# Local attention in a two-layer perceiver kernel: the shares of two of five sampling points move from VectorE to GpSimd

## The reference, cut to what matters

```python
loc_x = jnp.mod(ref + off + loc, sign_lens[:, None, None, None])
xg = loc_x / (key_len - 1) * 2.0 - 1.0
ix = ((xg + 1.0) * key_len - 1.0) / 2.0
x0 = jnp.floor(ix); dx = ix - x0
sk = 0.5 * (w0 * _gather_pad0(Kh, i0) + w1 * _gather_pad0(Kh, i1))   # w0 = 1 - dx, w1 = dx
sv = 0.5 * (w0 * _gather_pad0(Vh, i0) + w1 * _gather_pad0(Vh, i1))
scores = jnp.einsum('bhqd,bhqkd->bhqk', Qh / math.sqrt(HD), sk)
attn = jax.nn.softmax(scores, axis=-1)
```

## Time and profile before

| | us |
|---|---|
| median of three timed runs | 2892.89 (2889.31 to 2894.97) |
| profiled execution | 2884.54 |
| its span | 2882.6 |
| what lies around the span | 1.9 |
| VectorE busy, whole span | 1579.4 |
| GpSimd busy, whole span | 1008.7 |
| local attention, its loop over batches | from about 46 to 255 |

### The profile page before, as it was taken

How to read it: one execution, slowest core, us unless ns; L and a number is a source line. 1 busy time by engine, 2 the same in 40 slices (tenths; PEclk the granted TensorE clock), 3 DMA queues, 4 the chain that set the end, 5 groups by cost and what they waited for, 6 DMA issues and landing times. The chain is left out here.

```text
span 2882.6 us, 40247 instructions
## 1 busy us (share of the span) xinstructions
PE 2620.4 (91%) x15816; PEld 2126.3 (74%) x15816; DVE 1579.4 (55%) x2702; ACT 1056.8 (37%) x2114; POOL 1008.7 (35%) x486
## 2 busy tenths in 40 slices
PE   3887789997999999999999999999999868599898
PEld 2554478886888888888888888888888623377777
DVE  4895455443544544544444444444444469766775
ACT  2562223223443444443434434434344344222221
POOL 3561245444524313413432242143120037443342
PEclk7998789998999999999999999999999978799999
DMA  4000011112102111111111121121010000010110
GB/s 93 16 12 1 22 44 56 56 65 73 47 23 81 28 37 56 39 37 45 39 48 45 28 76 29 37 61 39 32 28 1 11 1 0 22 61 27 44 44 15
DMA packets 51501, 109.64 MB, mean 38 GB/s; under 512 B 21376, under 2 KB 26880, under 8 KB 46992
## 3 DMA queue, kind: packets, MB, share of 16 engines
q1 hardware_dynamic: 51344, 107.45, 12.3%
HBM read 106.05 MB, written 1.38 MB: 37 GB/s over the span
## 5 line engine op out<-in xcount | busy, mean ns | idle before, releaser
L1947 PE MATMUL img_ps<-cn,pt_hi 127*128 127x512 f32 x1536 | 552.0, 400 | 8.1 <-POOL cn L1666 8.0
L1948 PE MATMUL img_ps<-cn,pt_lo 127*128 127x256 f32 x1536 | 430.3, 280 | 0.0
L1664 POOL TENSOR_SCALAR ct<-staged 128x762 fp32r<-128x762 f32 x64 | 136.5, 2132 | 756.8 <-DMA staged<-in_ctx_t 526.7
L1947 PEld LDWEIGHTS img_ps<-cn,pt_hi 127*128 127x128 f32 x1536 | 290.0, 189 | 68.0 <-POOL cn L1666 8.2
L2073 DVE TENSOR_TENSOR pt_lo<-t_ps,pt_hi 127x512 fp32r<-127x512 f32 x384 | 241.4, 683 | 137.9 <-ACT pt_hi L2067 137.9
L1924 PE MATMUL s_ps<-ct,a_hi 128*128 128x508 f32 x768 | 312.2, 406 | 0.0
L1926 PE MATMUL s_ps<-ct,a_lo 128*128 128x508 f32 x768 | 301.4, 392 | 0.0
L1925 PE MATMUL s_ps<-ct,a_hi 128*128 128x508 f32 x768 | 301.3, 392 | 0.0
L1948 PEld LDWEIGHTS img_ps<-cn,pt_lo 127*128 127x128 f32 x1536 | 289.8, 189 | 0.0
L2130 ACT ACTIVATE prob<-s_ps,bias 128x1524 f32<-128x1524 f32 x128 | 196.6, 1536 | 142.4 <-DVE bias L2186 142.4
L1547 ACT ACTIVATE gate_e<-g_ps_e 128x512 f32<-128x512 f32 x136 | 81.4, 598 | 429.1 <-PE u_ps_e L1464 429.1
(11 more groups left out here) (327 smaller groups left out, 5784.9 us busy)
## 6 DMA issues: line engine op xcount, KB each, us to landing
staged<-in_ctx_n SPq DMA_DIRECT2D x64, 384.0 KB, 3.2
staged<-in_ctx_t SPq DMA_DIRECT2D x64, 381.0 KB, 3.2
up_raw_w<-in_up SPq DMA_DIRECT2D x17, 1024.0 KB, 4.8
down_raw_w<-in_down SPq DMA_DIRECT2D x17, 512.0 KB, 3.5
w_shared<-in_wq SPq DMA_DIRECT2D x7, 1024.0 KB, 6.2
w_shared<-in_wo SPq DMA_DIRECT2D x7, 1024.0 KB, 4.8
win<-in_ctx_near SPq DMA_DIRECT2D x16, 128.0 KB, 2.1
wv<-in_wv SPq DMA_DIRECT2D x1, 2048.0 KB, 8.7
```

What stands on the lines that cost most here:

```text
L1664: nc.gpsimd.tensor_scalar(hi, piece, 1.0, None, ALU.mult).then_inc(first.hi_done, 1)
L1947: nc.tensor.matmul(img_ps[:], pt_hi[0:IBLK, j, :], rows[0:IBLK, :, j, :], start=j == 0, stop=False)
L1948: last = nc.tensor.matmul(img_ps[:, D:2 * D], pt_lo[0:IBLK, j, :], rows[0:IBLK, 0, j, :], start=False, stop=j == IB - 1)
```

## The change

On GpSimd, the share of the last two points is formed by a new function `share_out`, behind `prepare(b + 1)` in the written order of batch b: it waits for `attn` of batch b (the sixth step of the semaphore `soft`) and for the sums of the same part of the batch before, and then issues the one multiply. VectorE issues the same function for the first three points alone. `share_done` becomes a list of two semaphores, one for each part. `attn` is no longer in the PSUM tile `marks` but in an SBUF array of its own, `attn0`; before VectorE writes it, it waits for GpSimd's share of the batch before. Two semaphores that counted single steps of VectorE, `spread_zeroed` and `half_kept`, become one, `kept_step`. What is computed is the same.

```diff
--- before.py
+++ after.py
@@ -400,7 +400,7 @@
     tent = [sb(f"tent{s}", [P, NK, TILES0, QW]) for s in range(2)]
     hit, share = sb("hit", [P, NK, TILES0, QW]), sb("share", [P, NK, TILES0, QW])
     spread = sb("spread0", [P, TILES0 * (WN + QT)])
-    score, shifted = sb("score", [P, PK]), sb("shifted", [P, PK])
+    score, shifted, attn = sb("score", [P, PK]), sb("shifted", [P, PK]), sb("attn0", [P, PK])
     turned = sb("turned0", [P, H0, S])
     total = sb("total0", [P, TILES0])
     inv = sb("inv0", [P, TILES0])
@@ -410,15 +410,16 @@
     w_ps = [ps(f"w0_ps{g}", [P, 4, P]) for g in range(2)]
     o_ps = ps("o_ps", [P, C, P])
     marks = ps("marks", [P, 512])
-    top, attn, weight = marks[:, 0:TILES0], marks[:, PK:2 * PK], marks[:, 2 * PK:3 * PK]
+    top, weight = marks[:, 0:TILES0], marks[:, 2 * PK:3 * PK]
     win_in = [sem(f"win_in{s}") for s in range(2)]
     kv_done, kt_kept, v_kept, q_masked = sem("kv_done"), sem("kt_kept"), sem("v_kept"), sem("q_masked")
     scored, dist_done, tent_step = sem("scored"), sem("dist_done"), sem("tent_step")
-    hit_done, soft, spread_zeroed = sem("hit_done"), sem("soft_step"), sem("spread_zeroed")
+    hit_done, soft = sem("hit_done"), sem("soft_step")
     exp_done = sem("exp_done")
-    share_done, summed, spread_done = sem("share_done"), sem("summed0"), sem("spread_done")
+    share_done = [sem(f"share_done{h}") for h in range(2)]
+    summed, spread_done = sem("summed0"), sem("spread_done")
     turned_done, turned_kept = sem("turned_done"), sem("turned_kept")
-    out_done, half_kept, out_kept = sem("out_done"), sem("half_kept"), sem("out_kept")
+    out_done, kept_step, out_kept = sem("out_done"), sem("kept_step"), sem("out_kept")
     SOFT = 6
     HALVES = NB // 2
 
@@ -426,6 +427,15 @@
 
     def part(buffer, h):
         return buffer[:, POINTS[h]].rearrange("p n i m -> p (n i m)")
+
+    def tiled(ap):
+        return ap.rearrange("p (a n) -> p a n", n=NK)
+
+    def share_out(eng, s, h):
+        points = POINTS[h].stop - POINTS[h].start
+        eng.tensor_tensor(share[:, POINTS[h]], tent[s][:, POINTS[h]],
+                          tiled(attn[:]).rearrange("p i n -> p n i")[:, POINTS[h]].unsqueeze(3)
+                          .broadcast_to([P, points, TILES0, QW]), ALU.mult).then_inc(share_done[h], 1)
 
     block = ctx.enter_context(nc.Block())
 
@@ -473,7 +483,7 @@
         def sums(b):
             pe.wait_ge(spread_done, b)
             for h in range(2):
-                pe.wait_ge(share_done, b * 2 + (h + 1))
+                pe.wait_ge(share_done[h], b + 1)
                 for n in range(NK)[POINTS[h]]:
                     last = nc.tensor.matmul(sum_ps[:].rearrange("p i m -> p (i m)"), k.ident,
                                             share[:, n].rearrange("p i m -> p (i m)"), start=n == 0, stop=n == NK - 1)
@@ -531,7 +541,7 @@
             pool.wait_ge(k.pos_in[0 if old is None else 1], H0 * 16)
             for h in range(2):
                 if old is not None:
-                    pool.wait_ge(share_done, old * 2 + (h - 1))
+                    pool.wait_ge(share_done[h], old)
                 points = POINTS[h].stop - POINTS[h].start
                 nc.gpsimd.tensor_tensor(
                     tent[s][:, POINTS[h]], small(k, "iota").rearrange("p (i m) -> p i m", m=QW)
@@ -546,6 +556,10 @@
                 b = i * 2 + s
                 if not (last and s == 1):
                     prepare(b + 1, 1 - s, None if first and s == 0 else b)
+                pool.wait_ge(soft, b * SOFT + 6)
+                if b > 0:
+                    pool.wait_ge(summed, b * 2)
+                share_out(nc.gpsimd, s, 1)
 
         pairs_of_batches(pool, body)
 
@@ -580,7 +594,7 @@
         for h in range(2):
             distances(0, 0, h)
             tents(0, 0, h)
-        act.wait_ge(spread_zeroed, 1)
+        act.wait_ge(kept_step, 1)
 
         def body(i, first, last):
             for s in range(2):
@@ -616,8 +630,8 @@
             if not isinstance(b, int) or b > 0:
                 dve.wait_ge(out_kept, b + 0)
             mask = small(k, "mask2")
-            nc.vector.tensor_scalar(kept[:], o_ps[:, :, 0:S], mask[:, 0:1], None, ALU.mult).then_inc(half_kept, 1)
-            dve.wait_ge(half_kept, b + 1)
+            nc.vector.tensor_scalar(kept[:], o_ps[:, :, 0:S], mask[:, 0:1], None, ALU.mult).then_inc(kept_step, 1)
+            dve.wait_ge(kept_step, b + 2)
             nc.vector.scalar_tensor_tensor(out=k.ctx_t[:, :, bass.ds(b * S, S)], in0=o_ps[:, :, S:2 * S],
                                            scalar=mask[:, 1:2], in1=kept[:], op0=ALU.mult,
                                            op1=ALU.add).then_inc(out_kept, 1)
@@ -630,9 +644,6 @@
 
         def by_tile(ap):
             return ap.unsqueeze(2).broadcast_to([P, TILES0, NK])
-
-        def tiled(ap):
-            return ap.rearrange("p (a n) -> p a n", n=NK)
 
         def body(i, first, last):
             for s in range(2):
@@ -661,21 +672,18 @@
                 dve.wait_ge(soft, at + 4)
                 nc.vector.reciprocal(inv[:], total[:]).then_inc(soft, 1)
                 dve.wait_ge(soft, at + 5)
-
-                nc.vector.scalar_tensor_tensor(out=tiled(attn), in0=tiled(weight), scalar=0.5, in1=by_tile(inv[:]),
+                if old:
+                    dve.wait_ge(share_done[1], b)
+                nc.vector.scalar_tensor_tensor(out=tiled(attn[:]), in0=tiled(weight), scalar=0.5, in1=by_tile(inv[:]),
                                                op0=ALU.mult, op1=ALU.mult).then_inc(soft, 1)
                 dve.wait_ge(soft, at + 6)
-                for h in range(2):
-                    if old:
-                        dve.wait_ge(summed, b * 2 + (h - 1))
-                    points = POINTS[h].stop - POINTS[h].start
-                    nc.vector.tensor_tensor(share[:, POINTS[h]], tent[s][:, POINTS[h]],
-                                            tiled(attn).rearrange("p i n -> p n i")[:, POINTS[h]].unsqueeze(3)
-                                            .broadcast_to([P, points, TILES0, QW]), ALU.mult).then_inc(share_done, 1)
+                if old:
+                    dve.wait_ge(summed, b * 2 - 1)
+                share_out(nc.vector, s, 0)
                 if old:
                     keep_outputs(b - 1)
 
-        nc.vector.memset(spread[:], 0.0).then_inc(spread_zeroed, 1)
+        nc.vector.memset(spread[:], 0.0).then_inc(kept_step, 1)
         pairs_of_batches(dve, body)
         keep_outputs(NB - 1)
```

## The result

The changed kernel takes 2910.89 us (median of 4 executions, 2907.52 to 2914.25) where the kernel before took 2891.24 us (median of 4 as well): a ratio of 1.0066, 95% interval 1.0048 to 1.0085, or 19.65 us more. The forecast was 2913 us, 20 us more. The profiled execution of the changed kernel took 2913.36 us, its span 2911.5.

The account below looks back on a forecast made before the run. Three tied paths at 10.9 us a batch were taken to bound the local attention; a new 12.65 us loop through GpSimd costs 19.0 us over 12 batches, plus 1 us for the clock: 2913 us, range 2899 to 2926.

Parts of the forecast that it names:

- The tie: Local attention, kernel before: VectorE, TensorE and ScalarE paths tie at 10.90 us a batch; removing 1.21 us from VectorE gains nothing.
- The queue: GpSimd's written order: masks and tents stand behind its wait and share, closing a new loop of 12.65 us a batch.
- (3): Part on GpSimd's queue place: loop of Exp, attn, GpSimd's share, masks, tent, Abs, spread, Relu, next Exp.
- The turns: Shares reading two SBUF operands exclude each other; VectorE goes first, 1.75 us, GpSimd's ends 1.80 to 1.94 us behind.
- Twelve steps: Local attention: 12 of 13 batch steps lengthen from 11.07 to 12.65 us, 19.0 us in all; the last stays.
- The clock: TensorE idles longer in each batch, so its clock may drop: 1 us added to the forecast.
- The rest of the kernel: Everything behind the local attention stage starts later and is otherwise the same.
- The signs: Expected in the trace: 12.6 us period, GpSimd's share 3.4 to 3.7 us, Exp wait grown 1.7 us, `hit` waiting.
- Side by side: Rival: both shares run without turns, loop 11.12 us a batch, 2894 us, no change that can be told; chance 0.12.
- GpSimd first: Rival: GpSimd's share runs before VectorE's, 11.94 us a batch, 2904 us; chance 0.08.
- A low clock: Rival: TensorE's clock falls and stays low, 15.7 us in half of the batches, 2931 us; chance 0.05.
- VectorE the only bound: Rival: VectorE alone bounds the stage, so the change saves 16 us, 2877 us; chance 0.03.

Follow-up runs that it names:

- edit B: Kernel before, with VectorE's share of the last two points formed for only 1 of 64 keys, nothing added elsewhere: 2888.54 us, ratio 0.9987.
- experiment 1: Changed kernel, with VectorE writing attn a second time into PSUM and its three-point share reading that copy: 2889.57 us, ratio 0.9997.
- experiment 3: Changed kernel, with a PSUM copy of attn for VectorE and the query masks made ahead of GpSimd's wait: 2888.43 us, ratio 0.9992.

## Why the prediction was right

*The tie.* Right in the main. The 1.21 us taken from VectorE gave nothing, as edit B shows with nothing added elsewhere. With VectorE's path out of the way the period is 10.82 us, not 10.9: the two others are 0.08 us shorter.

*GpSimd's multiply at 1.94 us.* Right, 1.94 us in experiment 1. The tent instruction with the same form of operands was the right row; the one with both operands dense (2.33 us) was too long. So was the estimate of 2.2 us from the Trainium skill's GPSIMD Engine Reference (Performance versus the Vector engine).

*The queue.* Right. The loop of (3) is the one in the trace, term by term: Exp to share 0.93, VectorE's share 1.76, GpSimd's end 1.80 behind it, masks 2.00, tent to Abs 2.85, Abs to Exp 3.24, together 12.58 us. Hold and masks were taken out of it one at a time.

*The turns.* Right in mechanism and in who goes first. The lead was smaller than I had worked out: 0.05 us, not 0.12, since GpSimd started 0.08 us behind the end of `attn` (101.49 to 101.57) where I had read 0.15 off a tent. GpSimd's share ended 1.80 us behind VectorE's, the lower of my two bounds, so the loop is 12.58 us, not 12.65: over 12 batches 0.8 us.

*Twelve steps.* Right: the thirteenth is 10.83 us. I had left it at the average of 11.07, 0.2 us too much.

*The clock.* The 1 us that I added for it was not there. TensorE was granted 0.86 in stretches like the last one above, as feared, but in eleven of the twelve steps its path stayed under the loop. Once it did not: from 214.75 to 227.50 us, with a granted clock of 0.74 in the stretch 210 to 223 us, the step is 12.75 us. The 12 steps average 12.60, so the clock costs 0.2 us. With that, 18.1 us in the loop where 20 were forecast.

*The rest of the kernel*, "starts later and is the same", held for the medians, 19.65 us against 18.1 in the loop. It did not hold for one profile against another: these two differ by 28.8 us. Of that, 4.0 lie ahead of the loop's steady part (the tents that wait for the positions' transfer begin at 81.93 us and not at 77.92), and 6.1 in the self attention behind it, which has no edit: 92.4 us with a granted clock of 0.79 against 86.3 us at 0.84. Whether part of these belongs to the change can't be told from one profile each; the medians leave room for about 1.6 us of it. That the median lies within 0.4 us of the forecast is luck: the loop fell 1.9 us short of it, and the interval of the ratio is 5 us wide to either side.

*The signs.* They came as forecast, but for one. VectorE's wait for the Exp grew from 0.27 (first line below, the kernel before) to as much as 2.03 us, and its busy time is 9.4 us a batch. But `hit` doesn't wait. The time that VectorE loses lies in two other waits, for TensorE's outputs and for the Exp (last two lines, the changed kernel from 97 to 260 us: us in total, times, longest):

```profile
196.20 0.20 DVE L659 TENSOR_REDUCE total<-marks 128x8 f32<-128x40 f32 x1 [0.27 <-ACT marks L596]
...
DVE kept L633 <- PE o_ps L507: 21.1, 13, 2.7
DVE total L670 <- ACT marks L610: 16.3, 13, 2.0
```

The rivals fell as follows. Side by side: GpSimd's record of 3.51 us, and experiment 1, which made it true and gave the 11.0 us that it had been priced at (11.12). GpSimd first: VectorE's share kept its 1.76 us. A low clock: the average of 12.60 us. VectorE the only bound: edit B and experiment 3.

## What to carry to other kernels

Before work is moved to an idle engine, write down what is queued behind it there and follow that to the next turn of the loop: an engine that was busy 6.8 of 10.9 us had no room for a held share of 3.5 us in front of its masks, though 6.8 + 3.5 is less than 10.9, and had it once they were put ahead of the wait. When two engines are to share one product, look at where every operand lies: a small array that both are to read, moved from PSUM to SBUF, made VectorE's own instruction hold GpSimd's, and a second copy of it in PSUM for VectorE ended that. And where several paths tie, take them down together or not at all; each edit alone may measure as nothing.

## What the runs showed of the hardware that I had not expected

The cost of a hold is regular enough to compute: in two kernels and two instructions it was what was left of VectorE's instruction less 0.14 us, in both (3.51 and 3.66 us). The scan of the earlier trace rows fits it: two reads of 2.33 us that overlap by 0.05 would end 4.61 us behind the scan that held them, and end 4.45 behind it. By the Trainium skill's SBUF page (Who interferes with whom) the loser waits for the whole of the other instruction; the trace agrees to within that 0.14 us.

In experiment 1 GpSimd's share began 0.07 us ahead of VectorE's and both kept their own time (1.94 and 1.75 us): with one of VectorE's operands in PSUM, the first to start holds nobody. Where GpSimd starts first and VectorE has both operands in SBUF, only the scan of the earlier trace rows shows what happens: VectorE's is then the one that is held. In the changed kernel's shares VectorE was first every time, by 0.05 us or a little less.

The start of the loop scatters: the second batch's share began at 84.70 to 88.95 us over the 13 profiles of kernels that do nearly the same work up to there; in the two compared above it goes by when the positions landed. A single profile can't settle a difference of 4 us in this kernel.
